# Prologue of a spectral layer: mode products scaled and placed straight from PSUM, the spectrum filled from four banks

## The reference, cut to what matters

```
x_ft = jnp.fft.fft2(xc, axes=(-2, -1))[:, :, :MODES, :MODES]        # MODES = 12
out_ft = jnp.einsum('bcmn,comn->bomn', x_ft, w_real + 1j * w_imag)
out_full = zeros.at[:, :, :MODES, :MODES].set(out_ft)
out = jnp.real(jnp.fft.ifft2(out_full, axes=(-2, -1)))
x = x + out
```

## Time and profile before

| | us |
|---|---|
| median of 3 runs | 2902.34 (2900.99 to 2904.39) |
| profiled execution | 2902.31 |
| its span, first to last instruction | 2900.5 |
| PE busy | 2473.0 (85%) |
| DVE busy | 2217.2 (76%) |
| ACT busy | 1384.5 (48%) |
| POOL busy | 1020.5 (35%) |

### The profile page before, as it was taken

How to read it: one execution, slowest core, us unless ns; L and a number is a source line. 1 busy time by engine, 2 the same in 40 slices (tenths; PEclk the granted TensorE clock), 3 DMA queues, 4 the chain that set the end, 5 groups by cost and what they waited for, 6 DMA issues and landing times. The chain is left out here.

```text
span 2900.5 us, 39672 instructions
## 1 busy us (share of the span) xinstructions
PE 2473.0 (85%) x12694; PEld 1847.7 (64%) x12694; DVE 2217.2 (76%) x3468; ACT 1384.5 (48%) x1812; POOL 1020.5 (35%) x1043
## 2 busy tenths in 40 slices
PE   0008999899898988999999999499899999979983
PEld 0005666566565656888888888376666666778872
DVE  6998888778787847888888888777676767527852
ACT  0107888788787875766666666222222222100000
POOL 0019888778787831000000000154444444300000
PEclk9999999999999998999999999799999999959997
DMA  9945999797787866777777776999999999549999
GB/s 384 388 161 206 342 338 340 285 337 285 280 337 288 319 256 255 273 288 275 288 274 286 275 286 247 356 382 416 400 416 400 416 391 398 158 136 370 421 420 411
DMA packets 244939, 926.87 MB, mean 320 GB/s; under 512 B 18009, under 2 KB 21593, under 8 KB 244442
## 3 DMA queue, kind: packets, MB, share of 16 engines
q1 hardware_dynamic: 205912, 796.12, 72.7%
q10 hardware_dynamic: 38898, 129.21, 11.1%
HBM read 527.85 MB, written 394.92 MB: 318 GB/s over the span
## 5 line engine op out<-in xcount | busy, mean ns | idle before, releaser
L1185 POOL TENSOR_TENSOR fi_square_sum<-fi_square_sum,fi_square 128x1024 f32<-128x1024 f32 x128 | 302.9, 2366 | 356.4 <-ACT fi_square L1151 356.4
L864 PE MATMUL ct_acc_ps<-ct_l_hi,ct_r_hi 128*128 128x512 f32 x1024 | 404.8, 395 | 26.7 <-DVE ct_r_lo L941 26.7
L669 DVE SCALAR_TENSOR_TENSOR pj_lr<-pj_v_ps,keep_b_val,pj_sig 128x1024 f32<-128x1024 f32 x256 | 328.7, 1284 | 118.2 <-ACT pj_sig L606 115.3
L865 PE MATMUL ct_acc_ps<-ct_l_lo,ct_r_hi 128*128 128x512 f32 x1024 | 404.5, 395 | 0.0
L866 PE MATMUL ct_acc_ps<-ct_l_hi,ct_r_lo 128*128 128x512 f32 x1024 | 404.4, 395 | 0.0
L1151 ACT ACTIVATE fi_square<-fi_x 128x1024 f32<-128x1024 f32 x128 | 135.5, 1058 | 513.8 <-DVE fi_x L1213 511.3
L507 POOL TENSOR_TENSOR front_ring<-front_ring,front_gn_shift 128x512 f32<-128x512 f32 x256 | 330.9, 1294 | 5.3 <-DVE front_ring L635 5.2
L606 ACT ACTIVATE pj_sig<-pj_g_ps,keep_b_gate 128x1024 f32<-128x1024 f32 x256 | 285.8, 1117 | 42.0 <-PE pj_g_ps L572 36.8
L1106 PE MATMUL fi_y_ps<-fi_scaled,keep_w_bd 128*128 128x512 f32 x512 | 271.9, 613 | 27.4 <-DVE fi_scaled L1196 26.9
L1196 DVE TENSOR_TENSOR fi_scaled<-fi_m,fi_s_ps 128x512 f32<-128x512 f32 x256 | 174.2, 681 | 132.0 <-DMA fi_m<-mixed_d 123.0
L527 POOL TENSOR_TENSOR front_ring<-front_ring,pj_guess 128x512 f32<-128x512 f32 x256 | 267.8, 1047 | 3.3 <-POOL pj_guess L521 1.6
(11 more groups left out here) (183 smaller groups left out, 5052.3 us busy)
## 6 DMA issues: line engine op xcount, KB each, us to landing
lr_d<-pj_lr SPq DMA_DIRECT2D x128, 1024.0 KB, 5.9
gate_d<-pj_gout SPq DMA_DIRECT2D x128, 512.0 KB, 6.9
ct_l<-lr_d SPq DMA_DIRECT2D x64, 1024.0 KB, 7.0
ct_r<-lr_d SPq DMA_DIRECT2D x64, 1024.0 KB, 9.0
mixed_d<-ct_o SPq DMA_DIRECT2D x64, 1024.0 KB, 5.0
fi_g<-gate_d SPq DMA_DIRECT2D x128, 512.0 KB, 14.6
fi_x<-in_x SPq DMA_DIRECT2D x32, 2048.0 KB, 17.2
fi_m<-mixed_d SPq DMA_DIRECT2D x128, 512.0 KB, 17.6
```

The costliest lines, as they stand in the source:

```text
L669: dve.scalar_tensor_tensor(out=out[:, :, RG * (m % 2):RG * (m % 2) + RG], in0=v_ps[:, :].rearrange("p (q i) -> p q i", i=RG), scalar=keep. ...
L864: pe.matmul(bank, high, l_hi[b][:, :, k, :], start=(k == 0), stop=False)
L865: pe.matmul(bank, high, l_lo[b][:, :, k, :], start=False, stop=False)
L1185: pool.tensor_tensor(square_sum[:, :, :], square_sum[:, :, :], square[:, :, :], ALU.add).then_inc(sum_done, 1)
```

## The change

The copy of `z_ps` to `z` and the tile `z` go. The four instructions that make `q` read `z_ps`, in PSUM, directly. The 24 transposes are put into four PSUM banks (4 to 7) with six pieces in each, instead of three with eight. `fill_spectrum` writes six columns per instruction and is called four times, twice by DVE (banks 0 and 1) and twice by ACT (banks 2 and 3): DVE still issues eight instructions, ACT eight in place of four. PE waits for two signals of ACT instead of one.

```
--- before.py
+++ after.py
@@ -1258,7 +1258,6 @@
         xr = mid.at("la", "xr", 118, [NM, NM])[0:C, :, :]
         xi = mid.at("la", "xi", 119, [NM, NM])[0:C, :, :]
         xm = mid.at("la", "xm", 120, [NM * NM, 2])
-        z = mid.at("la", "z", 122, [NM * NM, 2])[0:C, :, :]
         mean_in = t.sb("mean_in", [C, 1])
         sq_in = t.sb("sq_in", [C, 1])
         sums = t.sb("sums", [C, 2])
@@ -1275,7 +1274,8 @@
         f_ps = [ps[a][0:C, 0:NM * M2] for a in range(2)]
         s_ps = ps[2][0:C, :]
         z_ps = ps[3][0:C, 0:2 * NM * NM].rearrange("p (a r) -> p a r", r=2)
-        q_ps = [ps[4 + a][0:M2, :].rearrange("m (n o) -> m n o", o=C) for a in range(3)]
+        QN = M2 // 4
+        q_ps = [ps[4 + a][0:M2, 0:QN * C].rearrange("m (n o) -> m n o", o=C) for a in range(4)]
         w_loaded = t.sem("w_loaded")
         inv_loaded = t.sem("inv_loaded")
         loaded = [t.sem(f"loaded{b}") for b in range(XR)]
@@ -1308,8 +1308,8 @@
         def fill_spectrum(copy, a):
 
             for g in range(NG):
-                at = GP * g + 8 * a
-                last = copy(spectrum[GP * g:GP * g + M2, :, at:at + 8], q_ps[a].rearrange("m n o -> m o n"))
+                at = GP * g + QN * a
+                last = copy(spectrum[GP * g:GP * g + M2, :, at:at + QN], q_ps[a].rearrange("m n o -> m o n"))
             return last
 
         def copy_col(copy, i):
@@ -1359,11 +1359,11 @@
             last.then_inc(z_ready, 1)
             pe.wait_ge(q_in, 1)
             for n in range(M2):
-                last = pe.transpose(q_ps[n // 8][:, n % 8, :], q[:, n, :], keep.ident[0:C, 0:C])
+                last = pe.transpose(q_ps[n // QN][:, n % QN, :], q[:, n, :], keep.ident[0:C, 0:C])
             last.then_inc(q_ready, 1)
             pe.wait_ge(inv_loaded, 2 * DMA)
             pe.wait_ge(spectrum_dve, 2)
-            pe.wait_ge(spectrum_act, 1)
+            pe.wait_ge(spectrum_act, 2)
             for i in range(C // CB):
                 if i >= 4:
                     pe.wait_ge(col_dve if i % 2 == 0 else col_act, (i - 4) // 2 + 1)
@@ -1394,7 +1394,8 @@
 
             act.wait_ge(cleared, 2)
             act.wait_ge(q_ready, 1)
-            fill_spectrum(copy, 2).then_inc(spectrum_act, 1)
+            for a in (2, 3):
+                fill_spectrum(copy, a).then_inc(spectrum_act, 1)
             for i in range(1, C // CB, 2):
                 act.wait_ge(col_ready, i + 1)
                 copy_col(copy, i).then_inc(col_act, 1)
@@ -1434,9 +1435,8 @@
             dve.tensor_scalar(xm[C:P, :, 0], xi_f, v[:, 3:4], None, ALU.mult)
             dve.tensor_scalar(xm[C:P, :, 1], xr_f, v[:, 3:4], None, ALU.mult).then_inc(x_ready, 1)
             dve.wait_ge(z_ready, 1)
-            link(dve.tensor_copy(z[:, :, :], z_ps[:, :, :]))
-            zr = z[:, :, 0].rearrange("o (n m) -> o n m", m=NM)
-            zi = z[:, :, 1].rearrange("o (n m) -> o n m", m=NM)
+            zr = z_ps[:, 0:NM * NM, 0].rearrange("o (n m) -> o n m", m=NM)
+            zi = z_ps[:, 0:NM * NM, 1].rearrange("o (n m) -> o n m", m=NM)
             dve.tensor_copy(q[:, 0:NM, 0:NM], zr)
             dve.tensor_scalar(q[:, 0:NM, NM:M2], zi, -1.0, None, ALU.mult)
             dve.tensor_scalar(q[:, NM:M2, 0:NM], zi, -1.0, None, ALU.mult)
```

## The result

| | before | after |
|---|---|---|
| median of 22 runs each, us | 2904.38 (2900.99 to 2908.48) | 2900.43 (2896.29 to 2907.48) |
| profiled execution (its span), us | 2902.31 (2900.5) | 2896.74 (2894.9) |

The ratio is 0.9985, with a 95% interval of 0.9979 to 0.9991: 4.4 us less, between 2.6 and 6.1. The forecast was 4.7. The interval leaves out 1, so the change made the kernel faster; the saving is smaller than the 0.2% (5.8 us) that the prediction took for the least that can be told from no change. The absolute forecast, 2897.6 us, was 2.8 us too low: 2.0 of these come from its starting point, the median of three runs of the kernel before (2902.34), which became 2904.38 over 22.

The account below looks back on a forecast made before the run. The prediction took the closing DMA transfers as the bound, their start set by the prologue. Its terms, -3.66 - 1.07 = -4.73 us, took 2902.3 to 2897.6 us; range 2895.4 to 2901.2.

Parts of the forecast that it names:

- One to one to the end: From prologue to end of kernel: a microsecond saved in the prologue should be one microsecond at the end.
- Rival 3: At the kernel's end: it is set by something that does not move, 2902.3 us; chance 0.08.
- Part 1: Ahead of the fill: no z, q straight from PSUM; fills start 3.66 us earlier, POOL's memset last by 0.25 us.
- Rivals 1 and 2: Before the fill: DVE's memset waits for POOL's, 2900.8 us, chance 0.10; copies into q stand still, 2901.7 us, chance 0.06.
- Part 2: In the fill: four banks of six shorten DVE's eight fills to 4.48 us, a gain of 1.07 us.
- The clock: At L1371: the 1.2 GHz stretch of 4.5 us stays unchanged, zero; if gone, 2.2 us more are gained.
- Rival 4: At L1371: all of it runs at 1.2 GHz, 10.7 us more, net +6.0, 2908.3 us; chance 0.02.

Follow-up runs that it names:

- e4: The changed kernel with the 144 mode products made twice; ratio to the kernel before 1.0093 (1.0079 to 1.0108).
- e3: The kernel before with POOL's memset waiting for q_in in place of z_ready; ratio to the kernel before 0.9993 (0.9984 to 1.0001).
- e5: The changed kernel with the clearing of spectrum divided at channel 24 instead of 40; ratio to the kernel before 0.9984 (0.9974 to 0.9994).
- e6: The changed kernel with the clearing of spectrum divided at channel 56 instead of 40; ratio to the kernel before 0.9988 (0.9978 to 0.9998).
- e1: The kernel before with q made from PSUM and z gone, fills keeping three banks and eight columns; ratio to the kernel before 0.9982 (0.9973 to 0.9990).
- e2: The changed kernel with z put back and q made from it, keeping four banks of six columns; ratio to the kernel before 0.9996 (0.9987 to 1.0004).
- e8: The changed kernel with 11 unread products of 128 columns on PE ahead of L1371; ratio to the kernel before 0.9974 (0.9964 to 0.9985).

## Why the prediction was right

- **One to one to the end.** Right: the last stretch has one length within 1.3 us in thirteen profiles, and e4 moved the end by what it added. Rival 3 falls, as far as that scatter allows.
- **Part 1.** The step of 0.215 us between PSUM instructions and 0.94 us for four were met: 2583.37 to 2584.31. The fills start at 4.49 us for a forecast of 4.49. The prediction's remark that reading SBUF is the quicker way holds for L1441 to L1443 (one every 0.145 us in e3), but not for the SBUF pair L1432 and L1433, which it prices itself at 0.21; its sum does not use the remark. That POOL's memset becomes the last by 0.25 us is in the rows, and e5 and e6 confirm both its price and DVE's.
- **Rivals 1 and 2**, an instruction that waits for POOL. DVE's memset ran beside POOL's in full: it ended 3.21 us after `q`. The `q` instructions ran through. e3 shows that the standing still was real and POOL's doing, and e1 that the PSUM source lifts it.
- **Part 2.** 0.56 us per DVE fill as forecast, 4.50 in all for 4.48; ACT 3.93 for 3.93. e2 gives the part alone: 1.06.
- **The clock**, taken as unchanged. The low stretch was 2.9 us in place of 4.5 in the profiled execution. The kernels that leave L1371 alone scatter from 15.91 to 17.45 us, with the 16.68 of before in the middle, so zero is as good a value as these single profiles can give; that the change moves the clock by nothing on average is not shown. Here luck had its part: this term alone differs by 1.54 us between two profiles of the same changed kernel, a third of the whole saving. Rival 4, all of L1371 at 1.2 GHz, was seen in no profile.
- **The size.** Forecast -4.73 us, measured -4.72 at L1371's start and -4.4 (-2.6 to -6.1) end to end. The first agreement is earned term by term (3.66 for 3.66, 1.06 for 1.07). The second is closer than the interval of 1.8 us to either side can vouch for.
- **What can be told.** The prediction took 5.8 us as the least that tells from no change. With 22 runs of each kernel, 4.4 were enough for an interval that leaves out 1.

## What to carry to other kernels

A VectorE row that is far longer than its size asks (here 3.99 us for 144 elements) and ends with a GpSimd row can be a wait in disguise: no idle time is shown, the row itself is long. A run in which GpSimd starts later, as e3, shows whether it is. Change its source to PSUM, or start GpSimd's instruction later, and work out which of the parallel conditions then ends last before promising the whole row. Where a saving of a few microseconds lies below the scatter of the runs, read it from fixed points of the trace just around the change, and from the ratio only whether it agrees in sign and rough size.

## What the runs showed of the hardware that was not expected

- The record of a VectorE memset here is shorter than what it takes: 0.91, 2.62 and 4.33 us stand in the trace for 1.07, 3.21 and 5.34 us, and the missing part is shown as a gap called issue ahead of it. GpSimd's memset has no such gap: its record gives 0.85 ns per element, and the instruction that waited for it went on 0.1 us after the record's end.
- PE at a busy share of 100% on products of two columns kept the clock at 1.2 GHz for 31.9 us (63.6 in e4), and 4.2 us of products of 128 columns ahead of them did not raise it, while in e8 it rose some 2.5 us into products of that width, behind 2.7 us of transposes. What a rise needs is not shown by these runs.
